# Decoder layer, feed-forward stage: how the normed input gets its turned fp16 halves

## The chip, the cores and the metric

The program runs on one core of one Trainium2 chip. The metric is the device time of one execution in microseconds (us); lower is better. Inputs and outputs lie in the chip's main memory (DRAM) and are fp32.

## The reference

One decoder layer over 128 sequences of 128 tokens with 256 channels. Only its last third is touched here:

```python
x = x + attention(layernorm(x))                 # 16 heads
x = x + cross_attention(layernorm(x), context)  # 16 heads
x = x + ffn(layernorm(x))

def ffn(x, W_fc, ln_w, ln_b, W_proj):           # 256 -> 1024 -> 256
    h = einsum('btd,hd->bth', x, ternary(W_fc))
    h = gelu(h)
    h = layernorm(h) * ln_w + ln_b
    return einsum('bth,dh->btd', h, ternary(W_proj))
```

## The kernel before, in words

The program has three stages one after the other: setup (weights turned and made ternary), attention (self and cross), and the feed-forward `ffn`. Between attention and `ffn` the residual stream goes through a DRAM scratch, `x_scratch`. Each stage works on 32 groups; a group is `G` = 4 sequences of 128 tokens, with a token on each of the 128 partitions.

TensorE (PE) multiplies fp16 alone. So an fp32 value is split into a high half (the fp16 rounding, `HI`) and a low half (the rest, `LO`), and both are multiplied; the ternary weights are exact in fp16.

`ffn` is a software pipeline written out by hand: one body for each group `k`, with eight steps `s` = 0 to 7. Each engine has its own copy of the loop (`pe_body`, `act_body`, `dve_body`, `pool_body`, `sp_body`), its instructions run strictly in the order in which they are written, and semaphores tie the engines together. In the body of group `k` the engines work on four groups at once:

- group `n` = k+1 gets its input ready: statistics on VectorE (DVE), `rstd` on GpSimd (POOL), then `ffn_xn` = the normed input on ScalarE (ACT) in steps 2 and 3. In steps 4 and 6 PE turns `ffn_xn` (fp32) into the PSUM tile `xbk`, ACT writes its high half into `ffn_xhl`, and DVE writes the low half;
- group `k` itself: PE multiplies `ffn_xhl` with the first weight into `hbk` (line 1267), and ACT writes `hid` = Gelu of it (line 1149);
- group `q` = k-1: PE turns `hid` into `tbk` (line 1249), ACT and DVE write its halves `ghl`, and PE multiplies them with the second weight into `ybk` (line 1235). In step 3 ACT also writes `ffn_y` (`shift`, line 1167), to which POOL adds `ffn_xc`, the input with a bias;
- group `f` = k-2: DVE finishes `ffn_y`, and the SyncE queue (SP) stores it.

`ffn_src` and `ffn_xhl` have two buffers each, and `hbk` has two banks, so that `hbk` of step `s` waits for the `hid` of step `s`-2. PE waits for `ffn_xhl` ahead of `hbk` in steps 0 and 4 of a body:

```python
if s % 4 == 0:
    pe.wait_ge(xlo_ready, 2 * k + s // 4 + 1)
wait(pe, hid_ready, 8 * k + s - 1)
```

The attention stage makes its halves in the other order already: it writes the normed input into `xn`, its high half into `xs` on ACT (line 603), its low half into `xs` on POOL (line 514), and turns both on PE.

Of the kernel before, what the change touches and what calls it, by code (L numbers as in the profile page):

```python
# [12 lines left out]
ALU = mybir.AluOpType  # L13
# [3 lines left out]
P = 128  # L17
B, S, D = 128, 128, 256
# [1016 lines left out]
def ffn(nc, program, sh, x2_dram, out):  # L1035
# [10 lines left out]
    with ExitStack() as stack:  # L1046
# [6 lines left out]
        nmr = sb("ffn_nmr", [P, G])  # L1053
        xn = sb("ffn_xn", [P, G, D])
        xc = sb("ffn_xc", [P, 2, G, D])
        xhl = sb("ffn_xhl", [P, 2, 2, KT, T], F16)
        hid = sb("hid", [P, 2, G, F])
        hstats = sb("hstats", [P, G, 2, 6])
        hmv = sb("hmv", [P, 2, G, 2])
# [5 lines left out]
        held = sb("ffn_held_wait", [P, 2, G + 1])  # L1065
        hbk = ps("hbk", [P, 2, HF])
        tbk = ps("tbk", [P, 3, T])
        xbk = ps("xbk", [P, KT, 2 * S])
        ybk = ps("ybk", [P, G, D])

        loaded = [sem("even_loaded"), sem("odd_loaded")]
# [1 line left out]
        stats_done = sem("ffn_stats_done")  # L1073
        moments, var_ready, rstd_ready = sem("ffn_moments"), sem("ffn_var_ready"), sem("ffn_rstd_ready")
        nmr_ready, xn_ready, xc_ready = sem("ffn_nmr_ready"), sem("ffn_xn_ready"), sem("ffn_xc_ready")
        xT_ready, xhi_ready, xlo_ready = sem("ffn_xT_ready"), sem("ffn_xhi_ready"), sem("ffn_xlo_ready")
# [19 lines left out]
        def sp_body(sp, i):  # L1096
            for half in range(2):
                k = 2 * i + half
                if here(k - 2):
                    out_group = out_groups[k - 2]  # L1100
                    sp.wait_ge(y_ready, 4 * (k - 1))
                    sp.dma_start(out_group, y[:, half]).then_inc(stored[half], 16)
                if here(k + 1) and here(k + 3):
                    x2_group = x2_groups[k + 3]
                    sp.wait_ge(xc_ready, k + 2)
                    sp.dma_start(src[:, 1 - half], x2_group).then_inc(loaded[1 - half], 16)

        def pool_body(i):
            pool = nc.gpsimd
            for half in range(2):  # L1110
                k = 2 * i + half
                n, q = k + 1, k - 1
                if here(n):
                    pool.wait_ge(moments, n + 1)
                    pool.tensor_tensor(ve[:, :], mv[:, :, 1], sh.eps[:, :], ALU.add).then_inc(var_ready, 1)
                    pool.wait_ge(var_ready, n + 1)
                    wait(pool, xn_ready, 2 * n)
                    pool.tensor_tensor(rstd[:, :], ve[:, :], sh.mhalf[:, :], ALU.pow).then_inc(rstd_ready, 1)  # L1118
                if here(q):
                    pool.wait_ge(hmv_ready, 4 * (q + 1))  # L1120
                    pool.tensor_tensor(hve[:, :], hmv[:, 1 - half, :, 1], sh.eps[:, :], ALU.add).then_inc(hve_ready, 1)
                    pool.wait_ge(hve_ready, q + 1)
                    wait(pool, y_ready, 4 * (q - 1))
                    pool.tensor_tensor(hrstd[:, 1 - half], hve[:, :], sh.mhalf[:, :], ALU.pow).then_inc(hrstd_ready, 1)
                    pool.wait_ge(shift_ready, q + 1)
                    pool.wait_ge(xc_ready, q + 1)
                    pool.tensor_tensor(y[:, 1 - half], y[:, 1 - half], xc[:, 1 - half], ALU.add).then_inc(base_ready, 1)  # L1127
                if here(n):
                    pool.wait_ge(xn_ready, 2 * (n + 1))
                    wait(pool, base_ready, n - 1)  # L1130
                    pool.tensor_tensor(xc[:, 1 - half], src[:, 1 - half], sh.c2B[:, :].unsqueeze(1).broadcast_to([P, G, D]),
                                       ALU.add).then_inc(xc_ready, 1)

        def act_body(i):
            act = nc.scalar
            for half in range(2):
                k = 2 * i + half
                n, q = k + 1, k - 1
                for s in range(STEPS):
                    if here(q):  # L1140
                        act.wait_ge(gT_ready, 8 * q + s + 1)
                        wait(act, y_mm, 8 * (q - 1) + s + 1)
                        act.activation(ghl[:, HI, s], tbk[:, TURN_BANK[s]], ACT.Copy, scale=sh.lnwc[:, s:s + 1]).then_inc(ghi_ready, 1)  # L1143
                    if here(k):
                        act.wait_ge(h_mm, 8 * k + s + 1)
                        if s == 0:
                            wait(act, gT_ready, 8 * (k - 1))
                            wait(act, hmv_ready, 4 * (k - 1))
                        act.activation(hid[:, half, s // 2, s % 2 * HF:(s % 2 + 1) * HF], hbk[:, s % 2], ACT.Gelu).then_inc(hid_ready, 1)  # L1149
                    if s in (2, 3) and here(n):  # L1150
                        if s == 2:
                            act.wait_ge(nmr_ready, n + 1)
                            wait(act, xT_ready, 2 * n)
                        for b in (2 * s - 4, 2 * s - 3):
                            last = act.activation(xn[:, b], src[:, 1 - half, b], ACT.Identity, bias=nmr[:, b:b + 1], scale=rstd[:, b:b + 1])  # L1155
                        last.then_inc(xn_ready, 1)
                    if s in (4, 6) and here(n):
                        pair = s // 2 - 2
                        act.wait_ge(xT_ready, 2 * n + pair + 1)
                        if pair == 0:  # L1160
                            wait(act, h_mm, 8 * (n - 1))
                        act.activation(xhl[:, 1 - half, HI, :, 2 * S * pair:2 * S * (pair + 1)], xbk[:, :, :], ACT.Copy).then_inc(xhi_ready, 1)  # L1162
                    if s == 3 and here(q):
                        act.wait_ge(hnmr_ready, q + 1)
                        wait(act, stored[1 - half], 16 * (q // 2) if isinstance(q, int) else 16 * (i - 1 + half))
                        for b in range(G):
                            last = act.activation(y[:, 1 - half, b], sh.s2B[:, :], ACT.Copy, scale=hnmr[:, b:b + 1])  # L1167
                        last.then_inc(shift_ready, 1)

        def dve_body(i):  # L1170
# [11 lines left out]
            for half in range(2):  # L1182
                k = 2 * i + half
                n, q, f = k + 1, k - 1, k - 2
                for s in range(STEPS):
# [26 lines left out]
                    if here(q):  # L1212
                        dve.wait_ge(ghi_ready, 8 * q + s + 1)
                        dve.scalar_tensor_tensor(ghl[:, LO, s], tbk[:, TURN_BANK[s]], sh.lnwc[:, s:s + 1], ghl[:, HI, s],  # L1214
                                                 ALU.mult, ALU.subtract).then_inc(glo_ready, 1)
                    if s in (4, 6) and here(n):
                        pair = s // 2 - 2
                        dve.wait_ge(xhi_ready, 2 * n + pair + 1)
                        at = slice(2 * S * pair, 2 * S * (pair + 1))
                        dve.tensor_tensor(xhl[:, 1 - half, LO, :, at], xbk[:, :, :], xhl[:, 1 - half, HI, :, at], ALU.subtract).then_inc(xlo_ready, 1)  # L1220
                    if s > 3 and here(n + 1):
                        if s == 4:
                            dve.wait_ge(loaded[half], 16 * ((n + 1) // 2 + 1) if isinstance(n, int) else 16 * (i + 2))
# [2 lines left out]
        def pe_body(i):  # L1226
# [13 lines left out]
            for half in range(2):  # L1240
                k = 2 * i + half
                n, q, f = k + 1, k - 1, k - 2
                for s in range(STEPS):
                    if here(q):
# [3 lines left out]
                        for b in range(G):  # L1248
                            last = pe.transpose(tbk[:, TURN_BANK[s], b * S:(b + 1) * S], hid[:, 1 - half, b, s * P:(s + 1) * P], sh.ident[:, :])  # L1249
                        last.then_inc(gT_ready, 1)  # L1250
                    if s in (4, 6) and here(n):
                        pair = s // 2 - 2
                        pe.wait_ge(xn_ready, 2 * n + pair + 1)
                        wait(pe, xlo_ready, 2 * n + pair)
                        for kt in range(KT):
                            for b in range(2):
                                last = pe.transpose(xbk[:, kt, b * S:(b + 1) * S], xn[:, 2 * pair + b, kt * P:(kt + 1) * P], sh.ident[:, :])  # L1257
                        last.then_inc(xT_ready, 1)
                    if s == 0 and here(f):
                        second(f, FT - 1)  # L1260
                    if here(k):
                        if s % 4 == 0:
                            pe.wait_ge(xlo_ready, 2 * k + s // 4 + 1)
                        wait(pe, hid_ready, 8 * k + s - 1)
                        for part in (HI, LO):
                            for kt in range(KT):
                                last = pe.matmul(hbk[:, s % 2], xhl[:, half, part, kt, s // 2 * S:(s // 2 + 1) * S],  # L1267
                                                 sh.wfcT[:, kt, s % 2 * HF:(s % 2 + 1) * HF],
                                                 start=(part == HI and kt == 0), stop=(part == LO and kt == KT - 1))
                        last.then_inc(h_mm, 1)  # L1270
# [4 lines left out]
        with nc.Block() as block:  # L1275
            @block.sync
            def _(sp):
                for n in range(2):
                    sp.dma_start(src[:, n], x2_groups[n]).then_inc(loaded[n], 16)
                steps(sp, lambda i: sp_body(sp, i))  # L1280
                for n in range(2):
                    sp.wait_ge(stored[n], 16 * (NG // 2))

# [39 lines left out]
```

## Time and profile before

| what | value |
|---|---|
| median of three runs | 2684.58 us (2674.98 to 2684.99) |
| profiled execution: its own time | 2683.22 us |
| profiled execution: span from first to last instruction | 2681.4 us |
| PE busy, share of the span | 2346.2 us, 87% |
| DVE, ACT, POOL busy | 77%, 67%, 36% |
| mean granted TensorE clock | 0.964 of full speed |
| the `ffn` stage | from 2073.86 us to the end |

Busy shares are averages over the whole span; the stage that the change touches is the last 23% of it and is read by itself. L1257 stands for line 1257 of the program. PEld is the weight load of TensorE, which runs beside its matmuls. The time of an execution is 1.8 us more than its span.

### The profile page before, as it was taken

To read this page: it belongs to the slowest core of one execution; us is meant where nothing else is said; L and a number is where in the kernel's file an instruction comes from. 1 tells how busy PE (TensorE), PEld (TensorE's weight loads), DVE (VectorE), ACT (ScalarE), POOL (GpSimd) and SP (SyncE) were. 2 spreads that over 40 slices of the span, in tenths; PEclk is the share of its full clock that TensorE was granted. 3 is DMA by queue.
4 is the path that set the end of the run, shared out by engine and by line. 5 is a ranking of instruction groups with operands and counts; after the bars stand their busy time and mean duration, and the time that the engine had idled before them with its cause. 6 is when DMAs were issued, how large, how long until landed. Compare 5 with 4: busy or idle time off the path is not lost. (4 is left out here: it accounts for less than half of the span.)

```text
span 2681.4 us, 76693 instructions
## 1 busy us (share of the span) xinstructions
PE 2346.2 (87%) x30839; PEld 1583.6 (59%) x30839; DVE 2055.9 (77%) x4087; ACT 1785.1 (67%) x2480; POOL 960.4 (36%) x687
## 2 busy tenths in 40 slices
PE   3458999999999999999989999999865899999999
PEld 3234655665555565565655565565533677777777
DVE  5246888888787788888888888878653788888887
ACT  2245777777777777777766777776641777777776
POOL 0132343343343343344343344343221343343342
PEclk8679999999999999999999999999987999999999
DMA  2234454454454454444445444454321111111111
GB/s 84 47 59 80 93 100 85 94 104 85 91 98 81 90 94 99 90 92 93 91 92 100 88 92 96 87 93 96 58 51 35 49 55 55 63 55 55 62 55 40
DMA packets 184513, 209.74 MB, mean 78 GB/s; under 512 B 33104, under 2 KB 134864, under 8 KB 184272
## 3 DMA queue, kind: packets, MB, share of 16 engines
q1 hardware_dynamic: 181488, 203.55, 37.1%
q8 instruction: 218, 3.57, 0.6%
q10 hardware_dynamic: 2784, 2.43, 0.3%
q14 instruction: 23, 0.19, 0.0%
HBM read 54.87 MB, written 33.55 MB: 33 GB/s over the span
## 5 line engine op out<-in xcount | busy, mean ns | idle before, releaser
L580 ACT ACTIVATE prob<-exp_bank 128x1024 f32<-128x1024 f32 x512 | 523.6, 1023 | 203.2 <-PE exp_bank L844 196.4
L688 DVE TENSOR_REDUCE cross_mx<-score_bank 128x8 f32<-128x1024 f32 x256 | 310.8, 1214 | 121.2 <-PE score_bank L826 121.1
L688 DVE TENSOR_REDUCE self_mx<-score_bank 128x8 f32<-128x1024 f32 x256 | 311.1, 1215 | 105.5 <-PE score_bank L826 105.4
L514 POOL TENSOR_TENSOR xs<-xn,xs 128x1024 f16<-128x1024 f32 x64 | 136.1, 2127 | 573.2 <-ACT xs L603 573.2
L514 POOL TENSOR_TENSOR ahl<-attT,ahl 128x512 f16<-128x512 f32 x128 | 147.9, 1155 | 361.9 <-ACT ahl L585 361.9
L1267 PE MATMUL hbk<-wfcT,ffn_xhl 128*128 128x512 f16 x1024 | 264.4, 382 | 0.0
L1235 PE MATMUL ybk<-wpT,ghl 128*128 128x256 f16 x2048 | 260.2, 273 | 0.8 <-DVE ffn_y L1199 0.7
L720 DVE STREAM_TRANSPOSE out_bank<-out_bank 128x512 f32<-128x512 f32 x256 | 185.5, 725 | 85.0 <-PE out_bank L861 85.0
L1214 DVE SCALAR_TENSOR_TENSOR ghl<-tbk,lnwc,ghl 128x512 f16<-128x512 f32 x256 | 189.2, 739 | 73.5 <-ACT ghl L1143 71.8
L1235 PEld LDWEIGHTS ybk<-wpT,ghl 128*128 128x128 f16 x2048 | 200.1, 98 | 63.8 <-DVE ghl L1214 0.9
L1143 ACT ACTIVATE ghl<-tbk,lnwc 128x512 f16<-128x512 f32 x256 | 174.3, 682 | 75.4 <-PE tbk L1249 75.4
L884 PE MATMUL product_bank<-WT,ahl 128*128 128x256 f16 x1536 | 197.7, 281 | 9.6 <-ACT ctx_hl L612 4.8
L806 PE MATMUL exp_bank<-maskBT,pick 64*128 64x512 bf16 x1024 | 156.9, 385 | 52.5 <-ACT prob L580 35.4
L1149 ACT ACTIVATE hid<-hbk 128x512 f32<-128x512 f32 x256 | 152.6, 596 | 64.8 <-PE hbk L1267 57.5
L877 PE MATMUL product_bank<-self_xhl,WT 128*128 128x512 f16 x768 | 179.6, 384 | 10.7 <-ACT self_xhl L612 10.3
L806 PE MATMUL score_bank<-maskB,pick 64*128 64x512 bf16 x1024 | 158.5, 389 | 26.6 <-DVE cross_mx L688 14.8
L1175 DVE BATCH_NORM_STATS2 hstats<-hid 128x6 f32<-128x512 f32 x256 | 174.1, 680 | 1.7 <-ACT hid L1149 1.4
L884 PEld LDWEIGHTS product_bank<-WT,ahl 128*128 128x128 f16 x1536 | 144.0, 100 | 42.7 <-issue 9.8
L694 DVE SCALAR_TENSOR_TENSOR self_qk<-product_bank,bcol,self_qk 128x512 f16<-128x512 f32 x128 | 95.8, 750 | 85.6 <-ACT self_qk L570 83.7
L1249 PE MATMUL tbk<-ident,hid 128*128 128x128 f32 x1024 | 153.5, 273 | 0.8 <-ACT hid L1149 0.8
L826 PE MATMUL score_bank<-self_stk 48*128 48x128 f16 x2048 | 104.7, 223 | 53.7 <-DMA self_stk<-self_qk 28.1
L1127 POOL TENSOR_TENSOR ffn_y<-ffn_y,ffn_xc 128x1024 f32<-128x1024 f32 x32 | 75.5, 2359 | 200.3 <-ACT ffn_y L1167 200.3
(171 smaller groups left out, 5045.0 us busy)
## 6 DMA issues: line engine op xcount, KB each, us to landing
self_stk<-self_qk SPq DMA_DIRECT2D x768, 64.0 KB, 2.4
cross_stk<-cross_qk SPq DMA_DIRECT2D x768, 64.0 KB, 2.4
self_src<-in_x SPq DMA_DIRECT2D x32, 512.0 KB, 5.4
ctx_in<-in_ctx SPq DMA_DIRECT2D x32, 512.0 KB, 4.5
x_scratch<-xn SPq DMA_DIRECT2D x32, 512.0 KB, 5.5
ffn_src<-x_scratch SPq DMA_DIRECT2D x32, 512.0 KB, 3.8
out<-ffn_y SPq DMA_DIRECT2D x32, 512.0 KB, 3.0
self_stk<-self_negmT SPq DMA_DIRECT2D x64, 128.0 KB, 5.1
```

The lines of the kernel that those rows point to most:

```text
L514: nc.gpsimd.tensor_tensor(out, src, hi, ALU.subtract).then_inc(lo_ready, 1)
L580: act.activation(prob[:, p % 3], ebank[:, :, :], ACT.Exp, scale=EXP_SCALE).then_inc(b.exp_done, 1)
L688: dve.tensor_reduce(a.mx[:, 8 * m:8 * m + 8].rearrange("p (j r) -> p r j", r=2), sbank[:, :, :].rearrange("p r (j k) -> p r j k", j=4), AX ...
L720: dve.transpose(obank[:, 1], obank[:, 0]).then_inc(ch.o_turned, 1)
L806: pe.matmul(bank[:, r], sh.pick[rows, h], mask[rows, h], start=(h == 0), stop=False, skip_group_check=True)
L877: last = pe.matmul(pbank[:, n % 2], sh.WT[:, (b.wq, b.wk)[n // 2], wp, kt, n % 2 * P:(n % 2 + 1) * P], moving[:, part, kt, :], start=(k == ...
L884: last = pe.matmul(pbank[:, g // 2, g % 2 * D:(g % 2 + 1) * D], tokens[:, part, kt, g * S:(g + 1) * S], sh.WT[:, w, wp, kt, :], start=(k = ...
L1143: act.activation(ghl[:, HI, s], tbk[:, TURN_BANK[s]], ACT.Copy, scale=sh.lnwc[:, s:s + 1]).then_inc(ghi_ready, 1)
L1175: dve.bn_stats(hstats[:, s // 2, s % 2], hid[:, half, s // 2, s % 2 * HF:(s % 2 + 1) * HF]).then_inc(hstats_done, 1)
L1214: dve.scalar_tensor_tensor(ghl[:, LO, s], tbk[:, TURN_BANK[s]], sh.lnwc[:, s:s + 1], ghl[:, HI, s], ALU.mult, ALU.subtract).then_inc(glo_r ...
L1235: last = pe.matmul(ybk[:, b], ghl[:, part, t, b * S:(b + 1) * S], sh.wpT[:, t], start=(t == 0 and part == HI and b % 2 == 0), stop=(t == F ...
L1267: last = pe.matmul(hbk[:, s % 2], xhl[:, half, part, kt, s // 2 * S:(s // 2 + 1) * S], sh.wfcT[:, kt, s % 2 * HF:(s % 2 + 1) * HF], start= ...
```

## The change

The normed input is split into halves before it is turned, and the turn is made by one transposing DMA for each group, 512 KB of fp16, in place of eight fp32 turns on PE. ACT writes the high half `ffn_xs` from `ffn_xn` behind the second pair of norms in step 3, POOL writes the low half, and SP issues the transposing DMA into `ffn_xhl`. The two ACT and two DVE instructions that took the halves out of `xbk` are gone, and so is `xbk`. PE now waits once, ahead of step 0, for the whole group. SP's loop is written out for all groups; the other engines keep theirs. The diff, cut to its core:

```diff
-        xhl = sb("ffn_xhl", [P, 2, 2, KT, T], F16)
+        xs = sb("ffn_xs", [P, 2, G, D], F16)
+        xhl = sb("ffn_xhl", [P, 2, 2, G, KT, S], F16)
...
         def sp_body(sp, i):
             for half in range(2):
                 k = 2 * i + half
+                n = k + 1
+                if here(n):
+                    sp.wait_ge(xlo_ready, n + 1)
+                    wait(sp, h_mm, 8 * (n - 1))
+                    sp.dma_start(xhl[:, 1 - half].rearrange("p a b k s -> p (a b k) s"), xs[:, :, :, :].rearrange("p a b d -> p (a b d)"),
+                                 transpose=True).then_inc(x_turned, 16)
                 if here(k - 2):
                     out_group = out_groups[k - 2]
                     sp.wait_ge(y_ready, 4 * (k - 1))
                     sp.dma_start(out_group, y[:, half]).then_inc(stored[half], 16)
...
                     pool.tensor_tensor(hrstd[:, 1 - half], hve[:, :], sh.mhalf[:, :], ALU.pow).then_inc(hrstd_ready, 1)
+                if here(n):
+                    pool.wait_ge(xhi_ready, n + 1)
+                    pool.tensor_tensor(xs[:, LO], xn[:, :, :], xs[:, HI], ALU.subtract).then_inc(xlo_ready, 1)
+                if here(q):
                     pool.wait_ge(shift_ready, q + 1)
                     pool.wait_ge(xc_ready, q + 1)
                     pool.tensor_tensor(y[:, 1 - half], y[:, 1 - half], xc[:, 1 - half], ALU.add).then_inc(base_ready, 1)
...
-                    if s in (4, 6) and here(n):
-                        pair = s // 2 - 2
-                        act.wait_ge(xT_ready, 2 * n + pair + 1)
-                        if pair == 0:
-                            wait(act, h_mm, 8 * (n - 1))
-                        act.activation(xhl[:, 1 - half, HI, :, 2 * S * pair:2 * S * (pair + 1)], xbk[:, :, :], ACT.Copy).then_inc(xhi_ready, 1)
+                    if s == 3 and here(n):
+                        act.wait_ge(xn_ready, 2 * (n + 1))
+                        wait(act, x_turned, 16 * n)
+                        act.activation(xs[:, HI], xn[:, :, :], ACT.Copy).then_inc(xhi_ready, 1)
...
-                    if s in (4, 6) and here(n):
-                        pair = s // 2 - 2
-                        pe.wait_ge(xn_ready, 2 * n + pair + 1)
-                        wait(pe, xlo_ready, 2 * n + pair)
-                        for kt in range(KT):
-                            for b in range(2):
-                                last = pe.transpose(xbk[:, kt, b * S:(b + 1) * S], xn[:, 2 * pair + b, kt * P:(kt + 1) * P], sh.ident[:, :])
-                        last.then_inc(xT_ready, 1)
...
-                        if s % 4 == 0:
-                            pe.wait_ge(xlo_ready, 2 * k + s // 4 + 1)
+                        if s == 0:
+                            pe.wait_ge(x_turned, 16 * (k + 1))
```

On PE, from step 4 of a body written out ahead of the loop, the program before has these rows (`tbk` is the turned `hid`, `ybk` the second product):

```order
L1249 MATMUL tbk<-ident,hid 128x128 x4
L1257 MATMUL xbk<-ident,ffn_xn 128x128 x4
L1267 MATMUL hbk<-wfcT,ffn_xhl 128x512 x4
L1235 MATMUL ybk<-wpT,ghl 128x256 x8
L1249 MATMUL tbk<-ident,hid 128x128 x4
L1267 MATMUL hbk<-wfcT,ffn_xhl 128x512 x4
L1235 MATMUL ybk<-wpT,ghl 128x256 x8
L1249 MATMUL tbk<-ident,hid 128x128 x4
L1257 MATMUL xbk<-ident,ffn_xn 128x128 x4
L1267 MATMUL hbk<-wfcT,ffn_xhl 128x512 x4
```

The changed program has these in the same place:

```order
L1252 MATMUL tbk<-ident,hid 128x128 x4
L1262 MATMUL hbk<-wfcT,ffn_xhl 128x512 x4
L1238 MATMUL ybk<-wpT,ghl 128x256 x8
L1252 MATMUL tbk<-ident,hid 128x128 x4
L1262 MATMUL hbk<-wfcT,ffn_xhl 128x512 x4
L1238 MATMUL ybk<-wpT,ghl 128x256 x8
L1252 MATMUL tbk<-ident,hid 128x128 x4
L1262 MATMUL hbk<-wfcT,ffn_xhl 128x512 x4
```

Two packets of four turns are gone from each body, and nothing else on PE has moved.

On ACT, from `hid` of step 3 of such a body, the rows before are:

```order
L1149 ACTIVATE hid<-hbk 128x512
L1155 ACTIVATE ffn_xn<-ffn_src,ffn_nmr,ffn_rstd 128x256 x2
L1167 ACTIVATE ffn_y<-s2B,hnmr 128x256 x4
L1143 ACTIVATE ghl<-tbk,lnwc 128x512
L1149 ACTIVATE hid<-hbk 128x512
L1162 ACTIVATE ffn_xhl<-xbk 128x2x256
L1143 ACTIVATE ghl<-tbk,lnwc 128x512
L1149 ACTIVATE hid<-hbk 128x512
```

and in the changed program:

```order
L1159 ACTIVATE hid<-hbk 128x512
L1165 ACTIVATE ffn_xn<-ffn_src,ffn_nmr,ffn_rstd 128x256 x2
L1170 ACTIVATE ffn_xs<-ffn_xn 128x1024
L1175 ACTIVATE ffn_y<-s2B,hnmr 128x256 x4
L1153 ACTIVATE ghl<-tbk,lnwc 128x512
L1159 ACTIVATE hid<-hbk 128x512
L1153 ACTIVATE ghl<-tbk,lnwc 128x512
L1159 ACTIVATE hid<-hbk 128x512
```

The new high half stands ahead of the `ffn_y` rows and of `ghl` and `hid` of step 4; the two smaller halves behind `hid` of steps 4 and 6 are gone.

On SP, from the start of the stage, the changed program issues the transposing DMA of a group ahead of the store of an earlier one and of the next load:

```order
L1274 DMA ffn_src<-x_scratch 128x4x256 x2
L1103 DMA_TRANSPOSE ffn_xhl<-ffn_xs 128x16x128
L1112 DMA ffn_src<-x_scratch 128x4x256
L1103 DMA_TRANSPOSE ffn_xhl<-ffn_xs 128x16x128
L1112 DMA ffn_src<-x_scratch 128x4x256
L1103 DMA_TRANSPOSE ffn_xhl<-ffn_xs 128x16x128
L1112 DMA ffn_src<-x_scratch 128x4x256
L1103 DMA_TRANSPOSE ffn_xhl<-ffn_xs 128x16x128
L1108 DMA out<-ffn_y 128x4x256
L1112 DMA ffn_src<-x_scratch 128x4x256
```

Before, the same queue held only the `ffn_src` loads and the `out` stores, in the same order between themselves.

## Rows read from the trace of the kernel before

**Rows 1.** Busy time and count of each engine by stretch, granted clock, DMA share, GB/s.

```profile
core 0: us, PE busy (x) PEld busy (x) DVE busy (x) ACT busy (x) POOL busy (x), PEclk, DMA share, GB/s
2074.00:2086.00 12.00, 2.21 (x9) 1.72 (x10) 3.29 (x13) 2.67 (x5) 3.56 (x3) 0.50 0.27 87
2104.00:2662.98 558.98, 558.98 (x4165) 423.05 (x4164) 477.49 (x1241) 428.59 (x795) 215.39 (x180) 1.00 0.17 55
```

**Rows 2.** TensorE's groups of matmuls from 2104 to 2663 us.

```profile
L1267 PE MATMUL hbk<-wfcT,ffn_xhl 128*128 128x512 f16 x980 | 251.5, 379 | 0.0
...
L1257 PE MATMUL xbk<-ident,ffn_xn 128*128 128x128 f32 x240 | 36.0, 273 | 0.0
```

**Rows 3.** Timeline of TensorE over one body: start, duration, instructions.

```profile
2318.94 1.03 PE L1267 MATMUL hbk<-wfcT,ffn_xhl 128*128 128x512 f16 x4
...
2325.88 0.60 PE L1257 MATMUL xbk<-ident,ffn_xn 128*128 128x128 f32 x4
2326.32 1.03 PE L1267 MATMUL hbk<-wfcT,ffn_xhl 128*128 128x512 f16 x4
...
2330.67 0.60 PE L1257 MATMUL xbk<-ident,ffn_xn 128*128 128x128 f32 x4
2331.10 1.03 PE L1267 MATMUL hbk<-wfcT,ffn_xhl 128*128 128x512 f16 x4
...
2337.20 1.03 PE L1267 MATMUL hbk<-wfcT,ffn_xhl 128*128 128x512 f16 x4
```

**Rows 4.** Timeline of ScalarE, GpSimd and VectorE in the same body.

```profile
2325.27 1.08 ACT L1155 ACTIVATE ffn_xn<-ffn_src,ffn_nmr,ffn_rstd 128x256 f32<-128x256 f32 x2
2328.41 0.58 ACT L1149 ACTIVATE hid<-hbk 128x512 f32<-128x512 f32 x1
2328.89 0.59 ACT L1162 ACTIVATE ffn_xhl<-xbk 128x512 f16<-128x512 f32 x1
...
2330.52 2.36 POOL L1131 TENSOR_TENSOR ffn_xc<-ffn_src,c2B 128x1024 f32<-128x1024 f32 x1
2337.32 0.20 POOL L1115 TENSOR_TENSOR ffn_ve<-ffn_mv,eps 128x4 f32<-128x4 f32 x1 [4.44 <-DVE ffn_mv L1193]
...
2329.51 0.69 DVE L1220 TENSOR_TENSOR ffn_xhl<-xbk,ffn_xhl 128x512 f16<-128x512 f32 x1 [0.21 <-ACT ffn_xhl L1162]
```

**Rows 5.** Timeline of the attention stage: a normed input is split there.

```profile
1966.35 1.08 ACT L596 ACTIVATE xn<-cross_src,cross_nmr,cross_rstd 128x256 f32<-128x256 f32 x2
...
1967.46 1.06 ACT L603 ACTIVATE xs<-xn 128x1024 f16<-128x1024 f32 x1
...
1968.60 2.12 POOL L514 TENSOR_TENSOR xs<-xn,xs 128x1024 f16<-128x1024 f32 x1 [7.67 <-ACT xs L603]
```

**Rows 6.** DMA issues: count, KB of one, median us from issue to landing.

```profile
cross_stk<-cross_qk SPq DMA_DIRECT2D x768, 64.0 KB, 2.4
self_src<-in_x SPq DMA_DIRECT2D x32, 512.0 KB, 5.4
ffn_src<-x_scratch SPq DMA_DIRECT2D x32, 512.0 KB, 3.8
out<-ffn_y SPq DMA_DIRECT2D x32, 512.0 KB, 3.0
lnb_col<-in_L_ffn_ln_b SPq DMA_DIRECT2D x1, 4.0 KB, 4.0
```

**Rows 7.** Timeline of the start of the stage, and of the end of attention.

```profile
2068.16 2.34 POOL L533 TENSOR_TENSOR xn<-xn,cross_xb 128x1024 f32<-128x1024 f32 x1 [6.45 <-ACT xn L625]
2070.52 0.38 SPq L501 DMA_DIRECT2D x_scratch<-xn  x1
2081.14 2.07 ACT L1155 ACTIVATE ffn_xn<-ffn_src,ffn_nmr,ffn_rstd 128x256 f32<-128x256 f32 x4 [13.07 <-DVE ffn_nmr L1207]
2082.29 1.11 PE L1257 MATMUL xbk<-ident,ffn_xn 128*128 128x128 f32 x4 [15.27 <-ACT ffn_xn L1155]
2085.78 6.07 PE L1267 MATMUL hbk<-wfcT,ffn_xhl 128*128 128x512 f16 x16
2092.98 1.08 ACT L1155 ACTIVATE ffn_xn<-ffn_src,ffn_nmr,ffn_rstd 128x256 f32<-128x256 f32 x2
2099.82 1.03 PE L1267 MATMUL hbk<-wfcT,ffn_xhl 128*128 128x512 f16 x4
```

More of the change, by code:

```diff
@@ L1067, in ffn @@
         tbk = ps("tbk", [P, 3, T])
-        xbk = ps("xbk", [P, KT, 2 * S])
         ybk = ps("ybk", [P, G, D])
@@ L1075, in ffn @@
         nmr_ready, xn_ready, xc_ready = sem("ffn_nmr_ready"), sem("ffn_xn_ready"), sem("ffn_xc_ready")
[L1076 removed]
+        xhi_ready, xlo_ready, x_turned = sem("ffn_xhi_ready"), sem("ffn_xlo_ready"), sem("ffn_x_turned")
         h_mm, hid_ready, hstats_done, hmv_ready = sem("h_mm"), sem("hid_ready"), sem("hstats_done"), sem("hmv_ready")
@@ L1102, in sp_body @@
                     sp.dma_start(out_group, y[:, half]).then_inc(stored[half], 16)
-                if here(k + 1) and here(k + 3):
+                if here(n) and here(k + 3):
                     x2_group = x2_groups[k + 3]
@@ L1128, in pool_body @@
                 if here(n):
-                    pool.wait_ge(xn_ready, 2 * (n + 1))
+                    pool.wait_ge(xlo_ready, n + 1)
                     wait(pool, base_ready, n - 1)
@@ L1152, in act_body @@
                             act.wait_ge(nmr_ready, n + 1)
-                            wait(act, xT_ready, 2 * n)
+                            wait(act, xlo_ready, n)
                         for b in (2 * s - 4, 2 * s - 3):
@@ L1215, in dve_body @@
                                                  ALU.mult, ALU.subtract).then_inc(glo_ready, 1)
-                    if s in (4, 6) and here(n):
-                        pair = s // 2 - 2
-                        dve.wait_ge(xhi_ready, 2 * n + pair + 1)
-                        at = slice(2 * S * pair, 2 * S * (pair + 1))
-                        dve.tensor_tensor(xhl[:, 1 - half, LO, :, at], xbk[:, :, :], xhl[:, 1 - half, HI, :, at], ALU.subtract).then_inc(xlo_ready, 1)
                     if s > 3 and here(n + 1):
@@ L1250, in pe_body @@
                         last.then_inc(gT_ready, 1)
-                    if s in (4, 6) and here(n):
-                        pair = s // 2 - 2
-                        pe.wait_ge(xn_ready, 2 * n + pair + 1)
-                        wait(pe, xlo_ready, 2 * n + pair)
-                        for kt in range(KT):
-                            for b in range(2):
-                                last = pe.transpose(xbk[:, kt, b * S:(b + 1) * S], xn[:, 2 * pair + b, kt * P:(kt + 1) * P], sh.ident[:, :])
-                        last.then_inc(xT_ready, 1)
                     if s == 0 and here(f):
@@ L1266, in pe_body @@
                             for kt in range(KT):
-                                last = pe.matmul(hbk[:, s % 2], xhl[:, half, part, kt, s // 2 * S:(s // 2 + 1) * S],
+                                last = pe.matmul(hbk[:, s % 2], xhl[:, half, part, s // 2, kt],
                                                  sh.wfcT[:, kt, s % 2 * HF:(s % 2 + 1) * HF],
@@ L1279, in _ @@
                     sp.dma_start(src[:, n], x2_groups[n]).then_inc(loaded[n], 16)
-                steps(sp, lambda i: sp_body(sp, i))
+                for i in range(-1, NG // 2 + 1):
+                    sp_body(sp, i)
                 for n in range(2):
```

## The prediction, as it went on record

> **What bounds the kernel now.** The table of stretches comes first, because the change touches one stage only. From 2104 to 2663 us PE is busy for 558.98 of 558.98 us, at a granted clock of 1.00; DVE is busy for 477.49, ACT for 428.59, POOL for 215.39 us [rows 1]. So in the steady part PE alone sets the pace, and only PE's own work, or something that makes PE wait, can change the time. The timeline of PE gives the pace: `hbk` of step 0 starts at 2318.94 and again at 2337.20 us, so a body takes 18.26 us [rows 3]. The groups of PE say what a body consists of; `xbk`, the turns that go away, has 240 matmuls in that stretch, 8 for each of 30 bodies [rows 2]. At the start of the stage the bound is another one: PE waits there for one chain of small steps (norm, turn, halves), and its clock is granted at 0.50, which is the 1.2 GHz level, after 15.27 us without work [rows 1, 7].
>
> **What is removed from PE.** Durations of matmuls overlap (a packet of four turns shows 0.60 us), so a packet's price is the distance to the next start: 2325.88 to 2326.32 and 2330.67 to 2331.10, that is 0.44 + 0.43 = 0.87 us for a body [rows 3]. As PE never waits, all of it is on the path: 30 x 0.87 = **-26.1 us**. A body would take 17.39 us. The other engines allow that: 558.98 us hold 30.6 bodies, so DVE has 15.6 us of work in one, less 2 x 0.69 for the removed low halves = 14.2; ACT 14.0, less 2 x 0.59, plus 1.06 = 13.9; POOL 7.0 + 2.12 = 9.2 us [rows 1, 4, 5].
>
> **The new chain, and how late it may be.** I count from `hbk` of step 0 (2318.94). The second pair of norms is done at 2325.27 + 1.08 = 2326.35, 7.41 us later [rows 4], and nothing ahead of it has moved. The next two steps exist in the attention stage in the same shape: the high half starts 0.03 us after the norms and takes 1.06 us, the low half on POOL starts 0.08 us later and takes 2.12 us [rows 5]. POOL is free then: its next work, `ffn_y`, waits for ACT's `shift`. From a POOL instruction to SP's issue takes 0.02 us (2070.50 to 2070.52) [rows 7]. So the transposing DMA is issued at 7.41 + 0.03 + 1.06 + 0.08 + 2.12 + 0.02 = 10.7 us. PE wants it at 17.39 us, and needs some 0.1 us to see it. **A DMA that lands within 6.5 us of its issue is hidden; each us beyond costs 30 us in all**, because the next body's norms start from the late `hbk`.
>
> **How long does it take?** No transposing DMA stands in this trace. Plain DMAs of the same 512 KB land in 3.0 (`out`), 3.8 (`ffn_src`) and 5.4 us (`self_src`); a 64 KB one from SBUF to SBUF takes 2.4 [rows 6]. A lower bound is 3.0. For an upper bound by pieces: the 4 KB `lnb_col` load is 1024 pieces of four bytes and lands in 4.0 us [rows 6]; the transpose reads 2048 rows of 256 bytes, twice as many, so 8.0 us. I take **5.0**, near the slower of the plain ones, since both ends are in SBUF as for none of them. The choice is the weak point of this forecast: the limit of 6.5 lies between the two bounds. The Trainium skill leans to the same side in one place and against it in another. "Advanced Engine Details and Errata", section "X-Bar Transpose (TRN2)", says that transposing DMAs are about as fast as plain ones, which would leave the sum as it is. "VectorE: DVE Perf Modes", section "The three transpose paths", prices one square of 128x128 in 16 bits at 1309 ns by DMA against 390 ns on TensorE; a group has sixteen such squares.
>
> **What the start of the stage costs.** There PE waits, so the whole chain counts. Norms of group 0 end at 2083.21; + 0.03 + 1.06 + 0.08 + 2.12 + 0.02 gives the issue at 2086.5, and `hbk` starts at 2086.6 + L, L being the DMA's time, against 2085.78 before: 0.8 + L later [rows 7]. Group 1's norms follow the first `hbk` as before (they end at 2094.06 [rows 7]), now at 2094.86 + L; the same chain again (3.31 us) and L gives 2098.2 + 2L for the `hbk` that started at 2099.82 [rows 7]. So the start loses 2L - 1.6, **+8.4 us** at L = 5.0.
>
> **Moved and delayed work.** ACT's new 1.06 us stands ahead of `shift`, `ghl` and `hid` of step 4. That `hid` ended at 2328.99 and now ends at 2330.05; `hbk` of step 6, which needs its bank, would start at 2331.10 - 0.87 = 2330.23 [rows 3, 4]. The cover is 0.18 us, thin but there: 0. Without it each 0.1 us would cost 3 us in all. Behind it ACT regains the time, since the 0.59 us after that `hid` is gone [rows 4]. On POOL, `ffn_y` and `ffn_xc` come 1.7 us later; `ffn_xc` ended at 2332.88, and POOL then idled for 4.44 us [rows 4], so 0. On SP the store of group f, which was issued early in a body, waits behind the transposing DMA until 10.7 us into it; the buffer is written again a body later, so 0. The load of `ffn_src` is issued at some 15.6 us into a body instead of 13.9, and its statistics are a body and more away: 0. The DMA engines are 0.17 busy at 55 GB/s [rows 1]; 512 KB more for each body adds half of that.
>
> **Sum.** -26.1 + 8.4 = -17.7 us on a span of 2681.4: 2663.7. The profiled execution took 2683.22 us in all, 1.8 more than its span, so 2665.5; the median of the runs is 2684.58, 1.4 above it. Prediction: **2667 us**, 0.66% faster. As a function of L the change is -27.7 + 2L + 30 x max(0, L - 6.5).
>
> **Rivals.**
> 1. *The transpose is slower than the cover, and PE waits for it in each body.* It decides from L = 6.5; equal times at L = 7.0, and 0.5% slower at 7.4. At the bound of 8.0 it gives -27.7 + 16 + 45 = +33 us: 2718 us. At 10.0: -27.7 + 20 + 105 = +97, 2782 us. For it: the bound by pieces, and that a transpose cannot write its rows whole. Against it: all plain DMAs of this size stay under 6.5 [rows 6].
> 2. *The sixteen squares of a group are turned one after the other.* The nearest row is 2.4 us for 64 KB from SBUF to SBUF [rows 6]; a square is half of that, so 1.2 us each and L = 19.2: -27.7 + 38.4 + 381 = +392, 3076 us. Against it: it is a single instruction over sixteen DMA engines. By the skill's 1309 ns a square ("VectorE: DVE Perf Modes", "The three transpose paths") L would be 20.9 and the loss 446 us; nothing in this trace bears on it.
> 3. *ACT's order takes part of the gain.* If `hid` of step 4 is late by 0.3 us more than I count, PE loses 30 x 0.3 = 9 us: 2676 us. For it: a cover of 0.18 us. Against it: nothing else that ACT does up to there has grown.
>
> **Chances.** Forecast (L up to 6.5, gain over 0.5%): 0.44. Rival 1: 0.33, of it 0.08 within 0.5% and 0.25 slower. Rival 2: 0.10. Rival 3: 0.07, of it 0.04 within 0.5% and 0.03 faster. The rest, such as contention on SBUF or a lower granted clock behind new waits: 0.06, of it 0.01 faster, 0.01 the same, 0.04 slower. Faster by over 0.5%: 0.48; within 0.5%, about what a measurement of this kernel can tell from no change: 0.13; slower: 0.39. The forecast's own range is L from 3.0 to 6.5, 2663 to 2670, with the scatter of the runs (0.4%) 2656 to 2676. The range for all reaches from 2655 to L = 10, **2655 to 2782**: above it lie rival 2, some 0.06 of rival 1 and part of the rest.
>
> **What the profile of the changed kernel would show.** Right: the distance between `hbk` of step 0 in neighbouring bodies is 17.4 us; PE has no wait for the transposing DMA after the second body; its issue comes 10.7 us behind `hbk`, and it lands in 3 to 6.5 us; the first two bodies start 6 and 8 us later than before. Wrong by rival 1 or 2: a wait of PE on that DMA in each body, with a body of 10.8 + L. Wrong by rival 3: a wait of `hbk` in step 6 for `hid`, and no wait for the DMA. The forecast fails first on the DMA's time, then on the cover of 0.18 us.

## The result, and the profile after

The changed kernel takes 2654.79 us (median of six runs, 2648.68 to 2665.42); the kernel before, measured beside it, 2680.11 us (2667.22 to 2684.99). The ratio is 0.9906, with a 95% interval of 0.9884 to 0.9928. The forecast was 2667 us with a range from 2655 to 2782. So the direction was right and the gain larger than forecast, 25 us and not 18; the measured time lies 0.2 us below the range.

The first thing to read is where the stage begins. The load that opens the feed-forward stage is issued at 2058.52 us, and the span is 2646.9; before, it was issued at 2073.86 of 2681.4. **The stage itself went from 607.5 to 588.4 us, 19.2 less. The other 15.3 us between the two profiles lie ahead of it, in the attention stage, whose code is the same.** Much of that is the luck of two single executions: they stand at the upper end of the runs before and at the lower end of the runs after. More on it below.

The timeline of one body after the change, on PE, ACT, POOL and SP (start, duration, instructions):

```profile
2316.94 1.03 PE L1262 MATMUL hbk<-wfcT,ffn_xhl 128*128 128x512 f16 x4
...
2323.27 1.08 ACT L1165 ACTIVATE ffn_xn<-ffn_src,ffn_nmr,ffn_rstd 128x256 f32<-128x256 f32 x2
...
2324.46 1.06 ACT L1170 ACTIVATE ffn_xs<-ffn_xn 128x1024 f16<-128x1024 f32 x1
2325.59 2.14 POOL L1133 TENSOR_TENSOR ffn_xs<-ffn_xn,ffn_xs 128x1024 f16<-128x1024 f32 x1 [5.28 <-ACT ffn_xs L1170]
...
2327.59 0.58 ACT L1159 ACTIVATE hid<-hbk 128x512 f32<-128x512 f32 x1
...
2327.76 1.97 SPq L1103 DMA_TRANSPOSE ffn_xhl<-ffn_xs  x1
2328.23 1.03 PE L1262 MATMUL hbk<-wfcT,ffn_xhl 128*128 128x512 f16 x4
...
2334.37 1.03 PE L1262 MATMUL hbk<-wfcT,ffn_xhl 128*128 128x512 f16 x4
```

`hbk` of step 0 starts at 2316.94 and again at 2334.37: a body of 17.43 us, against 18.26 in [rows 3]. Over all bodies in which PE never waits it is 17.42 us on average. The transposing DMA is issued 10.82 us into the body. The views of the DMA issues and of the stretches add how long it takes and what it costs in traffic:

```profile
ffn_xhl<-ffn_xs SPq DMA_TRANSPOSE x32, 4.3
```

```profile
2120.00:2600.00 480.00, 480.00 (x3530) 354.39 (x3529) 393.27 (x1081) 381.40 (x687) 254.68 (x195) 1.00 0.35 91
```

It lands 4.3 us after its issue, 15.1 us into the body, some 2.3 us before PE asks. PE is busy for 480 of 480 us, as in [rows 1]: it never waits. The share of the DMA engines doubles to 0.35, where the forecast had added half; the bytes did grow by about half (91 GB/s against 58 in the same stretch before). A store of `ffn_y` now lands in 3.7 us and not 3.0, and PE feels none of it.

At the start of the stage (SP, PE):

```profile
2071.14 2.89 SPq L1103 DMA_TRANSPOSE ffn_xhl<-ffn_xs  x1
...
2075.52 5.95 PE L1262 MATMUL hbk<-wfcT,ffn_xhl 128*128 128x512 f16 x20 [23.85 <-DMA ffn_xhl<-ffn_xs]
...
2086.14 2.90 SPq L1103 DMA_TRANSPOSE ffn_xhl<-ffn_xs  x1
...
2090.44 1.04 PE L1262 MATMUL hbk<-wfcT,ffn_xhl 128*128 128x512 f16 x4 [2.75 <-DMA ffn_xhl<-ffn_xs]
```

`hbk` of group 1 starts 31.92 us into the stage; before it was 2099.82 - 2073.86 = 25.96 [rows 7]. The start lost 6.0 us. With 30 bodies, each 0.84 us shorter, that gives -25.2 + 6.0 = -19.2, all that the stage gained.

### The profile page after: what moved, and what is told of

Its sections match the earlier page's. It is cut to its first block and busy times, and to the rows that moved or that the text cites. A ratio compares the mean times of both kernels' runs of the same rounds, so it can differ in the third digit from the quotient of the medians.

```text
span 2646.9 us, 75785 instructions
## 1 busy us (share of the span) xinstructions
PE 2309.1 (87%) x30583; PEld 1548.1 (58%) x30583; DVE 2010.5 (76%) x4023; ACT 1782.4 (67%) x2448; POOL 1027.7 (39%) x719
## 5 line engine op out<-in xcount | busy, mean ns | idle before, releaser
L877 PE MATMUL product_bank<-self_xhl,WT 128*128 128x512 f16 x768 | 179.6, 384 | 10.9 <-ACT self_xhl L612 10.6
L1183 DVE BATCH_NORM_STATS2 hstats<-hid 128x6 f32<-128x512 f32 x256 | 174.3, 681 | 16.4 <-ACT hid L1159 16.3
L1262 PEld LDWEIGHTS hbk<-wfcT,ffn_xhl 128*128 128x128 f16 x1024 | 97.9, 98 | 97.3 <-DMA ffn_xhl<-ffn_xs 27.1
```

What stands on the lines that cost most here:

```text
L877: last = pe.matmul(pbank[:, n % 2], sh.WT[:, (b.wq, b.wk)[n // 2], wp, kt, n % 2 * P:(n % 2 + 1) * P], moving[:, part, kt, :], start=(k == ...
L1183: dve.bn_stats(hstats[:, s // 2, s % 2], hid[:, half, s // 2, s % 2 * HF:(s % 2 + 1) * HF]).then_inc(hstats_done, 1)
L1262: last = pe.matmul(hbk[:, s % 2], xhl[:, half, part, s // 2, kt], sh.wfcT[:, kt, s % 2 * HF:(s % 2 + 1) * HF], start=(part == HI and kt == ...
```

## The experiments

Each kernel ran beside the one before. For each I give the ratio and the length of the feed-forward stage in its profile (607.5 before, 588.4 after), which is the finer measure: the attention stage scatters by 4 to 5 us from run to run. The diffs show the lines that matter; tiles and waits that follow from them are left out.

**The changed kernel again.** No edit.

> The changed kernel once more, unaltered. Theory A (the part of the gain beyond the feed-forward stage is scatter of the untouched attention stage): the ratio to before comes nearer to 0.993, which is 19 us; the feed-forward stage, from its first load to the end, takes 588.4 us again to within 0.5 us, and the attention stage ends somewhere between 2055 and 2075 us in both kernels. Theory B (the change also shortens the attention stage, by where things lie in memory or by the longer SP program): the ratio stays at 0.990 to 0.991, some 25 us.

Ratio 0.9918 (0.9901 to 0.9936), stage 588.6 us. By the ratio the gain is 22 us, midway between theory A's 19 and theory B's 25, and the interval holds both.

**SP's loop written out, alone.**

```diff
-                steps(sp, lambda i: sp_body(sp, i))
+                for i in range(-1, NG // 2 + 1):
+                    sp_body(sp, i)
```

> The kernel before, with SP's loop in the feed-forward written out and nothing else. Theory A: no change, ratio 1.000 within 0.2%. Theory B, if the longer SP program is the cause: 6 us or more faster (ratio 0.998 or less) with the gain in the attention stage. A third way, that writing the loop out costs instruction loads: slower by a few us in the feed-forward stage, which took 607.5 us before.

Ratio 0.9993 (0.9981 to 1.0006), stage 607.6 us: the length of SP's program changes nothing in the stage, and by the interval it gives at most 5 us in all, not the 6 or more of theory B.

**The turns kept on PE as idle work.**

```diff
+                    if s in (4, 6) and here(n):
+                        pair = s // 2 - 2
+                        pe.wait_ge(xn_ready, 2 * n + pair + 1)
+                        for kt in range(KT):
+                            for b in range(2):
+                                pe.transpose(xbk[:, kt, b * S:(b + 1) * S], xn[:, 2 * pair + b, kt * P:(kt + 1) * P], sh.ident[:, :])
```

> The changed kernel, in which PE still turns the normed input into a spare PSUM tile that nobody reads (eight fp32 turns a body), as idle work. If the gain is PE's 0.87 us a body and nothing else: the feed-forward stage goes from 588.4 back to 588.4 + 26.1 = 614.5 us, which is 7 us more than before the change (607.5), with a body of 18.26 us. If the gain came from lighter work of DVE and ACT instead: the stage stays within a few us of 588.

Ratio 1.0029 (1.0016 to 1.0043), stage 613.8 us, body 18.26 us:

```profile
2306.92 1.03 PE L1269 MATMUL hbk<-wfcT,ffn_xhl 128*128 128x512 f16 x4
...
2325.18 1.03 PE L1269 MATMUL hbk<-wfcT,ffn_xhl 128*128 128x512 f16 x4
```

With PE's 0.87 us given back, the change is a loss of 6 us: its price at the start.

**Each group turned twice.**

```diff
+                    sp.dma_start(dump[:, 0], xs[:, :, :, :].rearrange("p a b d -> p (a b d)"), transpose=True).then_inc(x_turned, 16)
                     sp.dma_start(xhl[:, 1 - half].rearrange("p a b k s -> p (a b k) s"), xs[:, :, :, :].rearrange("p a b d -> p (a b d)"),
                                  transpose=True).then_inc(x_turned, 16)
```

> The changed kernel with each group turned by two DMAs of 512 KB, the first into a spare tile, the second into its place; PE waits for both. By the DMA engines' share (0.35 against 0.18, so 2.8 us of all sixteen for one transpose) both are in 4.3 + 2.8 = 7.1 us after the first issue. By the forecast's formula, 30 us for each us beyond 6.5 and 2 us for each us at the start: stage 588.4 + 18 + 5.6 = 612 us, with a wait of 0.6 us for the DMA in each body. If the cover is larger than counted, or two transposes overlap fully (4.3 to 6.2 us): 588 to 592 us. If they go one after the other whole (8.6 us): 588.4 + 63 + 8.6 = 660 us.

Ratio 0.9984 (0.9971 to 0.9997), stage 605.0 us. Its timeline of PE and SP over a body, and the DMA issue of the second copy:

```profile
2303.35 1.03 PE L1264 MATMUL hbk<-wfcT,ffn_xhl 128*128 128x512 f16 x4
...
2314.17 1.85 SPq L1104 DMA_TRANSPOSE ffn_dump<-ffn_xs  x1
...
2316.06 2.68 SPq L1105 DMA_TRANSPOSE ffn_xhl<-ffn_xs  x1
...
2321.05 1.03 PE L1264 MATMUL hbk<-wfcT,ffn_xhl 128*128 128x512 f16 x4
```

```profile
ffn_xhl<-ffn_xs SPq DMA_TRANSPOSE x32, 4.9
```

From the first issue to the landing of the second it is 1.9 + 4.9 = 6.8 us, 2.5 more than one copy takes. The body is 17.70 us, so it is 10.9 + 6.8, and the cover ends at 17.43 - 10.9 = 6.5 us, as forecast. A body lost 0.27 and not 0.6 us, since two copies overlap more than I counted; at 605.0 the stage misses the 612 us expected.

**Each group turned three times**, a second copy into the spare tile ahead of the real one.

> Each group turned by three DMAs of 512 KB, the last one into its place. Two of them were done 6.8 us after the first issue, 2.5 us more than one, with a body of 17.70 us. If the formula holds beyond the cover: 9.3 us, a body of 10.9 + 9.3 = 20.2 us, the stage at 588.4 + 30 x 2.8 + 2 x 5.0 = 682 us. If the engines save part of the time where PE waits (norms that come earlier): less than 670 us. If the clock of TensorE falls to its lower level behind waits of 3 us in each body: over 700 us.

Ratio 1.0299 (1.0284 to 1.0315), stage 694.5 us. The waits of PE for the DMA from 2110 to 2640 us (sum, times, longest), then PE's timeline behind one of them, then two stretches (the last three columns are granted clock, DMA share, GB/s):

```profile
PE hbk L1265 <- DMA ffn_xhl<-ffn_xs: 65.7, 25, 3.0
```

```profile
2374.95 1.89 PE L1265 MATMUL hbk<-wfcT,ffn_xhl 128*128 128x512 f16 x4 [2.63 <-DMA ffn_xhl<-ffn_xs]
2376.62 1.06 PE L1255 MATMUL tbk<-ident,hid 128*128 128x128 f32 x4
2377.48 1.26 PE L1265 MATMUL hbk<-wfcT,ffn_xhl 128*128 128x512 f16 x4
```

```profile
2366.00:2372.30 6.30, 6.30 (x50) 4.64 (x48) 6.21 (x16) 4.07 (x7) 4.21 (x2) 1.00 0.98 185
2374.90:2377.40 2.50, 2.46 (x8) 1.44 (x9) 0.01 (x1) 0.45 (x1) 0.63 (x1) 0.50 0.88 278
```

This is the rival of a slow transpose, made real: 25 waits of 2.6 us, and most bodies 20.0 to 20.4 us long, where the formula says 20.2. In 6 of 29 the body took 21.6 to 22.1: behind such a wait the clock was granted at 0.50, the 1.2 GHz level, for the next 2.5 us, and four `hbk` took 1.89 us in place of 1.03. That is most of the 12 us that the stage is over the 682 expected. While the three followed one another the DMA share was 0.98 on average; it reads 1.13 at 230 GB/s from 2369.8 to 2374.7 us, so over such short stretches it is rough, and that the DMA engines were full is not shown by it.

**Halves first, but turned on PE.** The transposing DMA is replaced by sixteen fp16 turns in steps 5 and 7 and two ACT copies:

```diff
+                    if s in (5, 7) and here(n):
+                        part = (s - 5) // 2
+                        pe.wait_ge(xhi_ready if part == HI else xlo_ready, n + 1)
+                        wait(pe, xbk_out, 2 * n + part)
+                        for b in range(G):
+                            for kt in range(KT):
+                                last = pe.transpose(xbk[:, KT * b + kt], xs[:, part, b, kt * P:(kt + 1) * P], sh.ident16[:, :])
+                        last.then_inc(x_turned, 1)
```

> The other part of the change alone: the normed input is split first, as in the changed kernel, but its fp16 halves are turned on PE (sixteen fp16 turns a body, in steps 5 and 7, taken out of PSUM by two ACT copies) and not by a DMA. If the gain is that PE has no turns left: sixteen fp16 turns of some 0.05 us cost about as much as eight fp32 turns of 0.109 us, the body is 18.2 to 18.3 us and the stage 612 to 616 us. If splitting first is itself a gain (lighter DVE): the body is nearer to 17.4 us and the stage below 595 us.

Ratio 1.0020 (1.0005 to 1.0035), stage 612.9 us, body 18.28 us. PE's timeline around one packet:

```profile
2309.44 0.61 PE L1262 MATMUL xbk<-ident,ffn_xs 128*128 128x128 f16 x8
2309.89 1.03 PE L1272 MATMUL hbk<-wfcT,ffn_xhl 128*128 128x512 f16 x4
```

Eight fp16 turns take 0.45 us, as long as four fp32 ones: twice the turns at half the price. (It is the products that PE makes in fp16 alone; the turns before ran in fp32.) Splitting first gains nothing by itself.

**The turns left out, and nothing else.** PE turns only groups 0 and 1; ACT and DVE go on taking halves out of an old `xbk`, so most of this kernel's output is of old data.

```diff
-                    if s in (4, 6) and here(n):
+                    if s in (4, 6) and isinstance(n, int) and 0 <= n < 2:
                         pair = s // 2 - 2
                         pe.wait_ge(xn_ready, 2 * n + pair + 1)
```

> The kernel before, in which PE turns the normed input of groups 0 and 1 only and leaves the turns out for the other 30; ACT and DVE still take their halves out of the PSUM tile, which then holds old values. There is no transposing DMA. If PE's turns are the whole price of a body: the stage goes from 607.5 to 607.5 - 26.1 = 581.4 us. For the attention stage, whose code is the same in all kernels and which ended at 2066 us on average in the changed kernel and at 2070 to 2071 in the one before: if a shorter feed-forward stage or less work of PE in it shortens attention, it ends near 2066 here too; if the transposing DMA does it, it ends near 2070.

Ratio 0.9916 (0.9897 to 0.9935), stage 592.2 us. This is a miss: the body is 17.76 us and not 17.39. The waits name why; the timeline shows the place (DVE and PE at the end of a body):

```profile
PEld ybk L1239 <- DVE ghl L1218: 11.7, 27, 0.4
```

```profile
2319.00 0.68 DVE L1224 TENSOR_TENSOR ffn_xhl<-xbk,ffn_xhl 128x512 f16<-128x512 f32 x1
...
2320.53 0.73 DVE L1218 SCALAR_TENSOR_TENSOR ghl<-tbk,lnwc,ghl 128x512 f16<-128x512 f32 x1
2320.53 0.60 PE L1253 MATMUL tbk<-ident,hid 128*128 128x128 f32 x4
...
2321.32 1.05 PE L1239 MATMUL ybk<-wpT,ghl 128*128 128x256 f16 x8 [0.19 <-DVE ghl L1218]
```

DVE's low half of the input, 0.68 us, stands in its queue ahead of `ghl` of step 7. At a pace of 18.26 us that was covered. At 17.39 it is not, and PE waits 0.4 us in each body. The changed kernel has moved that low half to POOL, and keeps no more than a few hundredths of such a wait (below).

**An idle transposing DMA in the kernel before**, one in each body, from a constant into a spare tile, with SP's loop written out.

```diff
+                if here(k + 1):
+                    sp.wait_ge(xn_ready, 2 * (k + 2))
+                    wait(sp, idle_turned, 16 * (k + 1))
+                    sp.dma_start(dump[:, :, :], sh.wfcT[:, :, :].rearrange("p k f -> p (k f)"), transpose=True).then_inc(idle_turned, 16)
```

> The kernel before, with SP's loop written out and one transposing DMA of 512 KB in each body that turns a constant into a spare tile and that no engine waits for. The stage stays at 607.5 us, since nothing waits (more than 609 us would mean that the DMA's traffic slows the engines or the other transfers). Attention ends near 2066 us if the transposing DMA, its code or its traffic, is what shortens it, and near 2070 if it is not.

Ratio 0.9997 (0.9983 to 1.0010), stage 606.3 us, the DMA again 4.3 us to landing. The DMA's traffic costs nothing here, and attention ends at 2072.0 on average: no sign that the DMA is what shortens it.

**The turns doubled** in the kernel before, each made twice into the same place.

> The kernel before, in which PE turns each normed input twice into the same place. The stage grows by 0.87 us a body for the 30 bodies where PE never waits, and by up to 3 us at the start, to 634 to 637 us. Attention ends near 2070 us if the work of the feed-forward stage has no part in it, and at 2074 or later if more work of PE there makes it longer.

Ratio 1.0104 (1.0080 to 1.0128), stage 635.5 us, body 19.13 us, 0.87 more again:

```profile
2311.47 1.03 PE L1267 MATMUL hbk<-wfcT,ffn_xhl 128*128 128x512 f16 x4
...
2330.61 1.03 PE L1267 MATMUL hbk<-wfcT,ffn_xhl 128*128 128x512 f16 x4
```

Attention ended at 2070.6 us on average, and not at 2074 or later.

**A shorter start.** Two DMAs of 256 KB, the first issued behind the high half, and the low half of groups 0 and 1 on DVE.

```diff
+                    wait(sp, h_mm, 8 * (n - 1))
+                    for part, ready in ((HI, xhi_ready), (LO, xlo_ready)):
+                        sp.wait_ge(ready, n + 1)
+                        sp.dma_start(xhl[:, 1 - half, part].rearrange("p b k s -> p (b k) s"), xs[:, part].rearrange("p b d -> p (b d)"),
+                                     transpose=True).then_inc(x_turned, 16)
...
+                    if s == 3 and isinstance(n, int) and 0 <= n < 2:
+                        dve.wait_ge(xhi_ready, n + 1)
+                        dve.tensor_tensor(xs[:, LO], xn[:, :, :], xs[:, HI], ALU.subtract).then_inc(xlo_ready, 1)
```

> The changed kernel with the chain at the start of the stage shortened: each half is turned by its own DMA of 256 KB, the high one issued as soon as ACT has written it, and the low half of groups 0 and 1 is written by DVE, which has nothing to do there, in place of POOL. If the start of the stage is the chain that was counted (norms, halves, DMA, twice): DVE takes some 1.2 us in place of 2.12, and the last DMA lands 3.0 us after its issue in place of 4.3, twice; the stage goes from 588.4 to 584 us, with a body of 17.39 us as before. If two DMAs cost more than one (each with its own fixed part and SP's issue): 588 us or more. The body must not change in either case, since the DMAs are hidden there.

Ratio 0.9891 (0.9875 to 0.9906), stage 585.5 us, the shortest of all, body 17.43 us. The start in its timeline (SP, DVE, PE):

```profile
2062.82 0.94 SPq L1278 DMA_DIRECT2D ffn_src<-x_scratch  x2
...
2073.27 2.73 SPq L1104 DMA_TRANSPOSE ffn_xhl<-ffn_xs  x2
2073.28 1.22 DVE L1227 TENSOR_TENSOR ffn_xs<-ffn_xn,ffn_xs 128x1024 f16<-128x1024 f32 x1 [3.23 <-ACT ffn_xs L1171]
...
2077.88 7.18 PE L1266 MATMUL hbk<-wfcT,ffn_xhl 128*128 128x512 f16 x20 [21.90 <-DMA ffn_xhl<-ffn_xs]
...
2091.82 1.04 PE L1266 MATMUL hbk<-wfcT,ffn_xhl 128*128 128x512 f16 x4 [0.70 <-DMA ffn_xhl<-ffn_xs]
```

DVE takes 1.22 us where POOL takes 2.12, and a DMA of half the size lands in 3.1. `hbk` of group 1 starts 29.0 us into the stage, 2.9 earlier than in the changed kernel. Some of the 4.4 expected went to PE's clock: the first twenty `hbk` took 7.18 us in place of 5.95, at a mean granted clock of 0.62 in place of 0.75.

**The changed kernel a third time**, for the attention stage.

> The changed kernel unaltered, a third time, for the attention stage alone. By the executions so far it ended at 2066.0 us on average in 12 runs of the changed kernel, and at 2070.0 in 35 of the one before, both with a scatter of 4 to 5 us. If that is scatter, the new runs come nearer to 2069; if something in the build shortens attention by 4 us, they stay at 2066. The feed-forward stage takes 588.4 to 588.6 us in both cases.

Ratio 0.9922 (0.9909 to 0.9936). Stage 591.2 us this time, outside the 588.4 to 588.6 expected, so it scatters by 2.8 us too. Nearly all of that is PE's clock behind its second wait at the start, which is as long as in the first profile (2.76 against 2.75 us):

```profile
2102.41 1.89 PE L1262 MATMUL hbk<-wfcT,ffn_xhl 128*128 128x512 f16 x4 [2.76 <-DMA ffn_xhl<-ffn_xs]
```

```profile
2102.40:2107.40 5.00, 4.99 (x16) 2.88 (x17) 1.51 (x3) 1.79 (x3) 0.83 (x1) 0.50 0.33 103
2090.40:2095.00 4.60, 4.56 (x30) 3.12 (x31) 2.81 (x8) 3.24 (x6) 0.87 (x1) 1.00 0.37 113
```

For 5.0 us the clock was granted at 0.50 (first row), where the first profile has 1.00 in the same place (second row); at half speed 5.0 us hold work for 2.5. With this profile's 591.2 taken off, attention ended at 2066.9 on average in 5 runs.

**The attention stage over all kernels.** A run's time less 1.8 us and less the stage of its kernel's profile leaves where attention ended. The means, with the number of runs:

| kernel | PE's work for each body of the stage | attention ended at (us) |
|---|---|---|
| before | 18.26 | 2070.6 (67 runs) |
| SP written out | 18.26 | 2068.9 (12) |
| idle transposing DMA | 18.26 | 2072.0 (12) |
| turns kept | 18.26 | 2072.6 (10) |
| halves on PE | 18.28 | 2071.4 (10) |
| turns doubled | 19.13 | 2070.7 (6) |
| changed, three times | 17.43 | 2066.2 (17) |
| turned twice | 17.43 and a wait | 2068.3 (10) |
| turned thrice | 17.43 and a long wait | 2063.9 (4) |
| shorter start | 17.43 | 2063.3 (5) |
| turns left out | 17.39 and a wait | 2063.5 (6) |

The error of each mean is 0.5 us for the first row and 1 to 3 us for the others, and the stage that is taken off comes from one profile and can itself be off by some 3 us. The kernels in which PE has less to do in the feed-forward stage end attention at 2063 to 2068 us, those in which it has as much as before or more at 2069 to 2073, with or without a transposing DMA, and however long the stage is (the one turned thrice has the longest). So some 4 us of the changed kernel's gain seem to lie in a stage that it does not touch: 4.5 us by these means, with an error of 1.2 that leaves out the scatter of the stage. The profiles, in which the load that opens the stage can be read directly, point the same way: it is issued at 2063.9 us on average in the seven profiles of kernels with less work for PE, and at 2073.4 in the six others, with an error of 3 us for the difference. This grouping was made after the numbers were seen, and against it stand the doubled turns, which moved nothing, and the kernels with SP written out (2068.9) and turned twice (2068.3), which lie next to each other from different groups. Where the tiles lie is not the cause, as the table has it: the kernel with the turns kept has the changed kernel's tiles and one more, and the one with the turns left out has those of before. What carries the gain there, no run shows.

## Why the mechanism was right, and which step of the sum failed

- **PE alone sets the pace, and its turns are 0.87 us a body: right in size.** Kept as idle work they give the 18.26 us back, doubled they cost 0.87 again. The measured body is 17.42 and not 17.39, so the term of -26.1 came out at -25.2 us. The missing 0.03 us fit PE waiting for DVE at the end of a body, too short to be listed as a wait:

```profile
2332.70 0.73 DVE L1222 SCALAR_TENSOR_TENSOR ghl<-tbk,lnwc,ghl 128x512 f16<-128x512 f32 x1
2333.01 0.60 PE L1252 MATMUL tbk<-ident,hid 128*128 128x128 f32 x4
2333.49 1.05 PE L1238 MATMUL ybk<-wpT,ghl 128*128 128x256 f16 x8
```

`ybk` starts 0.06 us after `ghl` ends and 0.45 to 0.48 us after `tbk`; in the last bodies, where DVE has no more input statistics to make, it is 0.43 us, and the body 17.38.
- **The other engines allow 17.39 us: right only because of something that the forecast priced at nothing.** It compared sums of busy time (DVE 14.2 of 17.39 us), which say nothing of what stands ahead of what. The kernel with only the turns left out shows that order counts: with DVE's low half left in its place the body is 17.76 us. By that run, moving it to POOL is worth 30 x 0.34 = 10 us of the change's gain. That the change did so was luck, not a reason of the forecast.
- **The new chain: right.** Issue at 10.7 us forecast, 10.82 measured; cover 6.5 us forecast, 6.5 measured with two copies; each us beyond it 30 us for the stage, as the body of 20.2 us with three copies shows.
- **The DMA's time: 5.0 us taken, 4.3 measured.** The weak point of the forecast was on the safe side, and the rivals in which the DMA is slow fall. What the Trainium skill says in "Advanced Engine Details and Errata", section "X-Bar Transpose (TRN2)", that a transposing DMA is about as fast as a plain one, agrees with this trace in the time to landing (4.3 against 3.7 to 5.6 us for plain ones of the same size). The Trainium skill's 1309 ns for one square of 128x128 ("VectorE: DVE Perf Modes", "The three transpose paths") is not a price that adds up over squares: sixteen of them would take 20.9 us, an estimate, and took 4.3.
- **The start of the stage: 8.4 us forecast, 6.0 measured.** Of the difference 1.4 comes from the DMA's time twice. The other 1.0 is that group 1's norms end 7.3 us behind the first `hbk` and not 8.3 as before: PE's clock was back at full level 4 us behind that `hbk` (first row, changed kernel), where it was still at the lower one before (second row), and a load of ACT's table that came behind the first `hbk` before now came ahead of it.

```profile
2079.50:2081.50 2.00, 1.97 (x10) 0.62 (x8) 1.51 (x4) 1.73 (x5) 0.00 (x0) 1.00 0.00 0
2086.00:2090.00 4.00, 4.00 (x10) 1.37 (x9) 2.58 (x10) 3.03 (x4) 1.22 (x2) 0.50 0.43 133
```

- **ACT's thin cover: right, and thinner.** `hid` of step 4 ends at 2328.17, and `hbk` of step 6 starts at 2328.23 without a recorded wait: 0.06 us where I counted 0.18. That it held is luck as much as reckoning.
- **The step that failed** is the last one of the sum, "-26.1 + 8.4 = -17.7 us on a span of 2681.4: 2663.7", with the median of 2684.58 set beside it. It held all that lies ahead of the stage fixed, and took its level from three runs. Six runs of the same kernel before have a median of 2680.11, 4.5 us lower. And attention ended another 4.5 us earlier in the changed kernel by the table, for a reason that stays open. The stage itself was not the trouble: its gain was forecast at 17.7 us and is 19.2, 18.9 and 16.3 in the three profiles, 18.1 on average. So the level and the attention stage make 9 of the 12 us between 2667 and 2654.8, and the rest is within the scatter of six runs. The range ended at 2655, since at its lower end it allowed for the DMA's best case and a little scatter, and for no gain elsewhere. That the measured median is 0.2 us outside and not inside is chance; the terms that were left out are not.

## What to carry to other kernels

Where one engine is busy without a gap, price what is taken off it by the distance between starts, and then look in the order of every other engine's queue for what will be late at the new pace; sums of busy time do not show it. A transposing DMA of this size took about as long to land as a plain one, and can take the turns off TensorE for nothing in a steady pipeline, as long as its chain is issued early enough; where a stage starts, the same chain is paid in full. Compare stages, not spans, when an untouched stage scatters by more than the effect.

## What the runs showed of the hardware that was not expected

- 512 KB of fp16 turned within SBUF took 4.3 us from issue to landing, 256 KB 3.1 us; a second one behind the first added 2.5 us. SP was held for 1.8 to 2.9 us by the issue.
- It costs the DMA engines more than plain traffic: it raised their share from 0.18 to 0.35 and the rate from 58 to 91 GB/s, so by this share the same bytes took them about 1.7 times as long (an estimate from these rounded figures). With three of them one behind the other the rate was 185 GB/s; in the stretch behind, with a plain store and load under way as well, 278 GB/s.
- A wait of 2.6 us in each body left TensorE's clock at 1.00 in most bodies and dropped it to 0.50 for some 2.5 us in 6 of 29. At the start of the stage the same wait of 2.8 us left it at 1.00 in one profile of the changed kernel and at 0.50 for 5.0 us in another.
- The attention stage, with the same code, seems to end some 4 us earlier in kernels that give TensorE less to do in the stage behind it. This stays open.
